# Second attention of a four-layer kernel: the front norm's centring moved from VectorE to GpSimd, and two tiles' gathers put into one stage

## What is computed

```
y = layer_norm(layernorm(x)) ; q, k = tanh(y Wq) pi/4, tanh(y Wk) pi/4 ; v = y Wv
heads = (cos q * cumsum(cos k * v) + sin q * cumsum(sin k * v)) / denom
x = layernorm(x) + heads Wo ;  x = x + gelu(layer_norm(x) W1 + b1) W2 + b2
```

## Time and profile before

| | |
|---|---|
| median of 3 runs | 2766.77 us (2761.01 to 2768.17) |
| profiled execution: its own time, its span | 2773.74 us, 2772.1 us |
| PE busy (share of the span) | 2417.6 us (87%) |
| DVE | 1825.7 us (66%) |
| ACT | 1343.4 us (48%) |
| POOL | 814.1 us (29%) |
| second attention, in the trace | from 1184 to 1805 us |

### The profile page before, as it was taken

One profiled execution on the slowest core, in us unless ns is written; L12 is line 12 of the kernel. 1 busy time (PEld: TensorE's weight loads), 2 busy tenths in 40 slices (PEclk: granted clock), 3 DMA queues, 4 the chain that ended last, 5 costly groups with the idle time before them and its releaser, 6 DMA issues. The chain is left out here.

```text
span 2772.1 us, 53723 instructions
## 1 busy us (share of the span) xinstructions
PE 2417.6 (87%) x20524; PEld 2154.1 (78%) x20524; DVE 1825.7 (66%) x3239; ACT 1343.4 (48%) x2061; POOL 814.1 (29%) x1194
## 2 busy tenths in 40 slices
PE   4999999952599999926787788879999999999999
PEld 3666666631599999914676677779999999999999
DVE  7666666663488888859999998367454454544544
ACT  1555555621477777623444444434454544545454
POOL 4555666326200000054666765500000000000000
PEclk7899999976799999957889999989999999999999
DMA  9994000002577777648555556044322222222222
GB/s 304 333 335 154 2 2 2 2 15 87 183 239 239 239 233 233 210 133 188 139 146 147 147 148 161 24 149 145 96 85 89 90 88 87 87 88 87 91 77 87
DMA packets 195374, 373.31 MB, mean 135 GB/s; under 512 B 28964, under 2 KB 105960, under 8 KB 194152
## 3 DMA queue, kind: packets, MB, share of 16 engines
q1 hardware_dynamic: 185816, 343.31, 40.4%
q0 software_dynamic: 9360, 27.27, 3.0%
HBM read 336.95 MB, written 100.66 MB: 158 GB/s over the span
## 5 line engine op out<-in xcount | busy, mean ns | idle before, releaser
L2319 DVE TENSOR_TENSOR e_h_lo<-e_h,e_h_hi 128x512 fp32r<-128x512 f32 x320 | 221.9, 693 | 300.7 <-ACT e_h_hi L2395 300.7
L2457 PE MATMUL e_h_ps<-e_yT_hi,e_w_hi 128*128 128x256 f32 x1280 | 362.4, 283 | 3.0 <-ACT e_h L2381 2.2
L2473 PE MATMUL e_y_ps<-e_w_hi,e_h_hi 128*128 128x256 f32 x1280 | 358.8, 280 | 2.4 <-DVE e_h_lo L2319 2.2
L2457 PE MATMUL e_h_ps<-e_yT_lo,e_w_hi 128*128 128x256 f32 x1280 | 358.3, 280 | 0.0
L2457 PE MATMUL e_h_ps<-e_yT_hi,e_w_lo 128*128 128x256 f32 x1280 | 358.1, 280 | 0.0
L2473 PE MATMUL e_y_ps<-e_w_hi,e_h_lo 128*128 128x256 f32 x1280 | 355.4, 278 | 0.0
L2473 PE MATMUL e_y_ps<-e_w_lo,e_h_hi 128*128 128x256 f32 x1280 | 355.2, 277 | 0.0
L2395 ACT ACTIVATE e_h_hi<-e_h 128x512 fp32r<-128x512 f32 x320 | 202.2, 632 | 276.9 <-DVE e_h L2314 220.6
L2381 ACT ACTIVATE e_h<-e_h_ps,e_b 128x512 f32<-128x512 f32 x320 | 218.9, 684 | 174.9 <-PE e_h_ps L2457 152.5
L2314 DVE TENSOR_TENSOR e_h<-e_h,e_spread 128x512 f32<-128x512 f32 x256 | 176.7, 690 | 133.6 <-ACT e_h L2381 132.5
L462 DVE TENSOR_REDUCE a_top<-a_ring 128x2 f32<-128x1024 f32 (+3 forms) x256 | 204.1, 818 | 73.5 <-PE a_ring L651 72.1
(11 more groups left out here) (370 smaller groups left out, 6782.4 us busy)
## 6 DMA issues: line engine op xcount, KB each, us to landing
e_w<-in_w SPq DMA_DIRECT2D x78, 1024.0 KB, 5.6
e_spread<-share_store SPq DMA_DIRECT2D x512, 128.0 KB, 2.8
a_keys<-rows_store SPq DMA_DIRECT2D x128, 256.0 KB
a_queries<-rows_store SPq DMA_DIRECT2D x86, 256.0 KB
a_running_hidden<-rows_store SPq DMA_DIRECT2D x42, 256.0 KB
e_xs<-sorted_x SPq DMA_DIRECT2D x39, 256.0 KB, 4.8
sorted_y<-e_ys POOLq DMA_DIRECT2D x39, 256.0 KB, 5.7
e_stage_buf<-in_w_all SPq DMA_DIRECT2D x10, 512.0 KB, 3.9
```

The costliest lines, as they stand in the source:

```text
L2319: dve.tensor_tensor(h_parts[q % 2][1][:, :], h[:, q % 2, :], h_parts[q % 2][0][:, :], ALU.subtract).then_inc(h_lo.sem, h_lo.tick())
L2457: last = pe.matmul(h_ps[q % 2][:, cols], l, r, start=(m == 0), stop=(m == len(ops) - 1))
L2473: last = pe.matmul(y_ps[n][:, 0:D], h_parts[q % 2][a][:, n * P:(n + 1) * P], w2[b][:, c, :], start=(q == 0 and m == 0), stop=(q == CH - 1 ...
```

## The change

Three edits. (1) `refine_front` on GpSimd gets four instructions behind its Newton iteration: a product into newton[:, 0], its negation into centre, the same again into minus, each with a wait for the one before. (2) `centre_of` is gone from VectorE, in the start and in stage 5; `back(s, "add")` gets a wait for the centring of its own batch. (3) The gathers of tiles 2 and 3 are both issued in stage 6 (the seventh) in place of one in stage 6 and one in stage 7. A helper on TensorE is renamed.

```
+        product, centred = sig("product", 2), sig("centred", 2)
...
                 rsqrt_refine(pool, refined, s, inverse[:, :, ours], half[:, :, ours], newton[:, :, ours], three_halves[:, :, 0:TB])
+                for out, by in ((centre, twice), (minus, rstd)):
+                    pool.tensor_tensor(newton[:, 0, ours], mv[:, ours, 0], by[:, ours], ALU.mult).then_inc(product.sem)
+                    pool.wait_ge(product.sem, product.at(1 if out is centre else 2, s))
+                    pool.tensor_scalar(out[:, ours], newton[:, 0, ours], -1.0, None, ALU.mult).then_inc(centred.sem)
+                    pool.wait_ge(centred.sem, centred.at(1 if out is centre else 2, s))
...
-                if c >= 4 and live(s + 3):
+                if c in (4, 5) and live(s + 3):
                     gather(s + 3, range(c - 4, c - 3))
+                if c == 6 and live(s + 3):
+                    gather(s + 3, range(2, TB))
...
-            def centre_of(s):
-                ours = slice(s * TB, (s + 1) * TB)
-                dve.wait_ge(refined.sem, refined.at(12, s))
-                dve.scalar_tensor_tensor(out=centre[:, ours], in0=mv[:, ours, 0], scalar=-1.0, in1=twice[:, ours], op0=ALU.mult,
-                                         op1=ALU.mult).then_inc(centred.sem)
-                dve.scalar_tensor_tensor(out=minus[:, ours], in0=mv[:, ours, 0], scalar=-1.0, in1=rstd[:, ours], op0=ALU.mult,
-                                         op1=ALU.mult).then_inc(centred.sem)
...
                     dve.wait_ge(x_plus.sem, x_plus.at(TB, s))
+                    dve.wait_ge(centred.sem, centred.at(2, s))
...
-                if c == 5 and s >= 1 and live(s + 2):
-                    centre_of(s + 2)
```

More of the change, by code:

```diff
@@ L1378, in attention1_phase @@
         stat_step, seeded, refined = sig("stat_step", 2 * TB + 3, SET_UP), sig("seeded", 3), sig("refined", 12)
-        centred = sig("centred", 2)
+        product, centred = sig("product", 2), sig("centred", 2)
         znF, trF, yF_full, yF_hi, yF_lo = sig("znF", TB), sig("trF", KC), sig("yF_full", KC), sig("yF_hi", KC), sig("yF_lo", KC)
@@ L1713, in _ @@
             low_weights(0)
-            centre_of(0)
             combine(1, LEFT)
@@ L1720, in _ @@
             low_weights(1)
-            centre_of(1)
             combine(2, LEFT)
@@ L1727, in _ @@
             low_weights(2)
-            centre_of(2)
             for n in range(STAGES):
@@ L1884, in _, with matrix_product @@
             TERMS = ((0, 0), (0, 1), (1, 0))
-            def product(out, pairs):
+            def matrix_product(out, pairs):
                 ops = [(l[a], r[b]) for l, r in pairs for a, b in TERMS]
@@ L1912, in value @@
                     pe.wait_ge(turned.sem, turned.at(2 * (n - 1)))
-                product(v_ps[n % 2][:, :], [([w[:, k, c * P:(c + 1) * P] for w in wv],
+                matrix_product(v_ps[n % 2][:, :], [([w[:, k, c * P:(c + 1) * P] for w in wv],
                                              [y[:, k, :] for y in front_T[s % 2]]) for k in range(KC)]).then_inc(v_done.sem,
@@ L1933, in find_angles @@
                     pe.wait_ge(tanhs.sem, tanhs.at(2 * s + 1))
-                product(h_ps[0:ROWS, :], [([w[:, k, q, :] for w in wqk],
+                matrix_product(h_ps[0:ROWS, :], [([w[:, k, q, :] for w in wqk],
                                            [y[:, k, :] for y in front_T[s % 2]]) for k in range(KC)]).then_inc(angles.sem,
@@ L1953, in up @@
                 c = u % FC1
-                product(h_ps[:, :], [([w[:, k, c * P:(c + 1) * P] for w in w1],
+                matrix_product(h_ps[:, :], [([w[:, k, c * P:(c + 1) * P] for w in w1],
                                       [y[:, k, :] for y in back_T]) for k in range(KC)]).then_inc(up_done.sem, up_done.tick())
```

## The result

The changed kernel takes 2750.01 us, the median of 5 runs (2746.9 to 2755.78), against 2766.77 us: a ratio of 0.9943, with a 95% interval of 0.9932 to 0.9955. That is 16.8 us faster, where 14.2 had been worked out. A second measurement against the kernel before gave 0.9945 (0.9925 to 0.9965). The profiled execution took 2746.9 us with a span of 2745.2. In it the second attention, from VectorE's first combine to the first transfer of the next expert layer, takes 1778.34 - 1189.66 = 588.7 us, against 1805.16 - 1198.06 = 607.1: 18.4 us less. Nearly all of the rest, 8.4 us, arises before the second attention, in code that the change doesn't touch.

What follows compares the result with a forecast made beforehand. VectorE was taken to set turns 2 to 4, with POOL bounding stage 3 to stage 0 after the change. Terms -2.2, -0.6, +1.7, +5.7, +3.9, +3.8, +1.9 sum to 14.2 us: 2766.8 to about 2753, range 2743 to 2765.

Steps and rivals of the forecast that it cites:

- start: Before the pipeline: gathers behind the centring in POOL's list come 1.12 us later for each of two batches; loss 2.2 us.
- turn 0: Left half of the combine: a streak, not a gather, stands beside it, so it ends later; loss 0.6 us.
- turn 1: Right half of the combine: tile 3 is there in time, but it is held until POOL's streak ends; gain 1.7 us.
- turn 2: VectorE reaches stage 6 4.4 us earlier, POOL's 4.62 us rest goes, POOL then bounds; gain 5.7 us.
- turn 3: Left half of the combine falls among the gathers, POOL's 2.19 us rest goes, POOL then bounds; gain 3.9 us.
- turn 4: Taken to have the same pattern as the turn before it; gain 3.8 us.
- turn 5: No gathers here; VectorE's 2.05 us hold at the centring goes and POOL has rests after it; gain 1.9 us.
- The centring on POOL: Four small POOL instructions behind the Newton iteration, 0.28 us each, 1.12 us a batch; upper bound 2.13 for a held one.
- Rival 3: Centring dear on POOL: tensor_scalar held or slow at 2.13 us each, 4.8 us a centring; 2775 us, chance 0.09.
- The joined streak: POOL's streaks of stages 7 and 0, with no gather left between them, join into one of 7.5 us.
- Rival 1: Shorter hold: right half of the combine slips between two POOL instructions, bound by its data; gain 21 us, 2746, chance 0.17.
- Rival 2: POOL does not get its rest back; mainly the wait for tile 3 is saved; gain 4 us, 2763 us, chance 0.22.

## Why the prediction was right, and where it wasn't

The median is within 3 us of the forecast, and the sum's method (one turn at a time, gain only up to the next wait) held in kind. Several steps were off and in part cancelled. Taken from stage 1 to stage 1, where the steps were counted:

| step | forecast | measured |
|---|---|---|
| start | -2.2 | -1.4 |
| turn 0 | -0.6 | +1.1 |
| turn 1 | +1.7 | +0.4 |
| turn 2 | +5.7 | +5.7 |
| turn 3 | +3.9 | +6.0 |
| turn 4 | +3.8 | +3.5 |
| turn 5 | +1.9 | +2.3 |
| turn 6, and the tail | 0 | +2.2, -1.3 |
| sum | 14.2 | 18.4 (profiled) |

- *The centring on POOL*: right in the start, short by 0.5 us in the turns (1.60 against 1.12), where a product is held; net of the hold it takes over from the heads it is 1.1. The tensor_scalar took 0.22 to 0.23 us (once 0.54), where a tensor_tensor's 0.20 had been taken and 2.13 had been the upper bound. Rival 3 falls. The Trainium skill (GPSIMD Engine Reference, "Engine selection") would have kept the work on VectorE. For the bare instruction the traces agree with it, for the kernel they don't: beside POOL's streaks the same two instructions cost VectorE 4.4 us.
- *The start*: right in kind, oversized. Stage 1 of turn 0 came 1.4 us later, chunk 0 itself 0.9, not 2.2. Doubling the centring there shows the mechanism: 6.46 us of waiting for the rows.
- *Turn 0*: wrong in sign. The step that put a streak "not a gather" beside LEFT was right (1.17 and 1.90 us, against 0.87 and 2.52, so 0.3 less), but a hold in the old place had simply been replaced by a similar one. Where the other 0.8 us of turn 0 come from isn't known.
- *Turn 1*: "now tile 3 is there in time" was wrong. RIGHT waited another 2.37 us for it at 1358.31. The landing time was the mis-sized term: the last of four bunched gathers landed 8.58, 8.36 and 8.34 us after its instruction began in turns 1, 2 and 3, where 7.25 had been taken from turn 2 (one to a stage, turns 1, 3 and 4 have 6.68, 7.91 and 7.67).
- *Turns 2 to 4*: 65, 67 and 64 us were forecast and 64.8 measured in each, so turn 3 gained 2.1 us more than forecast. The forecast took away each turn's own rest of POOL, 4.62 and 2.19 us; three equal turns say that the length hangs on something they share. The account of RIGHT was half right. "RIGHT without a DMA wait but with one held instruction of 3 to 5 us" failed: it waits 2 to 4 us for rows, and its held instructions take 1.0 to 1.6 us where 0.48 is bare. Yet its last tile is held to the end of stage 0's streak: in turn 2 1425.10 against 1424.82, and VectorE goes on at 1426.49. That is 1.67 us behind the streak's end, for which 2.16 had been taken. Data and streak end within a microsecond of each other, so either reading gave nearly the same time. The joined streak doesn't exist as one: POOL pauses 0.8 us for the hidden half.
- *Rival 1* (RIGHT slips between two instructions of the streak and is bound by its data) was nearer than its 0.17. RIGHT does wait for data, and in turn 1 it does slip through: the instruction of 1358.31 is free while the next one of the streak runs on. "Held until POOL's unbroken streak ends" was taken from the one place behind a gather and used for all. It is so behind a gather (4.40, 4.59, 5.59 and 6.21 us beside instructions of 1.3) and not elsewhere. The Trainium skill (SBUF — State Buffer, "Who interferes with whom") says of the ports that VectorE and GpSimd share that the one that issues first gets them "for the whole instruction", in a sentence on VectorE's two-port modes. By length the traces agree with one instruction where no gather stands ahead, and show the whole streak where one does. The gain of 16.8 us lies between the forecast's 14.2 and this rival's 21.
- *Rival 2* (POOL keeps its rest) fell: behind the centring no rest over 1 us is left up to stage 0's streak in turns 2, 3 and 4, and the rest of 4.62 us before the hidden half is 0.80.
- *What the account lacked*: the prediction costed the centring and the gathers as separate terms. The runs show that where each two-input instruction meets POOL's list decides, and that a shift of 0.9 us (0.63 to 1.54 ahead of a streak) turns 4.40 us into 0.15. Nothing in the working would have forecast that 0.8 us less on POOL costs 9 us. And the errors of single turns are large beside that of the sum (turn 0 +1.7, turn 1 -1.3, turn 3 +2.1, turn 6 +2.2, the tail -1.3) and cancel in part; in the profiles the sum is 4.2 us off, in the medians 2.6. That the forecast came out right for a change at such a point was partly luck.

Open: why a gather in front lengthens the hold; why the hold then already begins about 0.6 us before the streak's recorded start (0.63 in the earlier trace rows, 0.56 in the run with the centring alone on POOL); what turn 6 gained its 2.2 us by; and whether the kernel with POOL only delayed, joined with the bunched gathers, would match the change. That wasn't run. None of the versions that were run beats the change.

## What to carry to other kernels

Look for tiny VectorE instructions with long durations, and read POOL's timeline beside them: if both their inputs are in SBUF, what must change is where they stand relative to POOL's unbroken streaks, those directly behind a gather above all. Moving them or moving POOL did it here. Idle instructions with a PSUM operand weren't held either; that wasn't tried on the centring itself. Before taking a wait away, ask what else that wait is hiding, and whether the data behind the next wait come any sooner; a part that gains 5 us alone and another that gains nothing may gain 16 together, and the other way round. With engines that meet at such points, try small shifts of order on the chip rather than trust a sum of instruction costs.

## What the runs showed of the hardware that was not expected

- A VectorE instruction with both inputs in SBUF is held through several GpSimd instructions in a row where a gather instruction stands directly in front of them (35 holds of 35): 6.21 us for a pair beside a streak of four, 4.36 to 4.41 beside three. Without a gather in front it was free at the end of one GpSimd instruction (109 of 109), as 0.96 us for the product that elsewhere took 4.51. Gather instructions of GpSimd hold nothing (0.87 and 0.90 us for a pair beside them), and an instruction with one operand in PSUM was never held (150 to 160 ns in 36).
- The holding goes both ways in small: beside VectorE's two-input instructions the last Newton instruction of turns 2 to 5 took 1.10 to 1.11 us in the changed kernel and 1.10 to 1.17 in the kernel before, instead of 0.20, and in the start one took 2.13.
- PE's granted clock was higher in the shorter turns. Over turn 3 it stood at 0.97 in the changed kernel (54.20 us of PE busy in 64.9, stage 0 to stage 0) and at 0.89 in the slowest version, with the centring held and the combine in stage 1 (59.27 us for the same 338 matmuls in 75.1). It doesn't follow the holds themselves: from stage 1 to stage 1 the kernel with the gathers alone has 0.95 with its holds, the one with POOL delayed 0.93 without the centring's. Whether the slower matmuls cost time isn't shown.
- An added delay of 1.1 us on an engine made the kernel 8.6 us faster.
